# Eight gathers, then a look at the slab counter: GpSimd's rounds in layers two and three

## The chip, the cores and the metric

The kernel is one program on one core of a Trainium2 chip. Its time is the device time of one execution in microseconds (us), from the first to the last instruction. The kernel before takes 3301.0 us, the median of three runs (3299.79 to 3303.86).

## The reference

A graph of 6250 nodes (padded to 49 tiles of 128) and 200,000 edges with weights, features of 128. First a gated graph network of three layers, all in float32:

```python
for l in range(L):                      # L = 3
    m = x @ weight[l]
    msg = m[src] * edge_weight[:, None]
    agg = jax.ops.segment_sum(msg, dst, num_segments=N)
    x = _gru_cell(agg, x, w_ih, w_hh, b_ih, b_hh)
```

The result is added to the input and normalised over the features; then a second network of three layers, `relu((x + agg) @ W.T + b)` with an unweighted sum over the edges, is applied, added and normalised again.

## The kernel before

The sum over the edges is written as a product with a dense matrix. Layer one builds that matrix (weighted in `adj_w`, float32; counts in `adj_h`, float16) strip by strip, writes it to HBM and uses it at once. That takes the first 1090 us. The three count layers of the second network are the last 820 us. The change lies between them, in layers two and three.

The nodes are cut into 14 groups of 448 columns. In layers two and three the first 12 groups (`DENSE`) are dense: for each group TensorE multiplies the 49 tiles of node features `Y` with 49 pieces of the matrix, 128 x 448 float32, accumulating in one PSUM bank. A float32 product stands in the profile as two matmul records, so a group has 98 records of line 923 and the gates of a group 12 more (lines 933 to 936). The matrix of a group comes in four slabs (13, 12, 12 and 12 tiles, so 26, 24, 24 and 24 records). SyncE loads a slab into its buffer when the slab of the group before in that buffer has been used: the last matmul of each slab adds one to the semaphore `s_used` (line 925), and SyncE waits for it (line 511). `s_used` starts at 4. The order of TensorE is: the slabs of group g+1, then the gates of group g, then the slabs of group g+2. ScalarE copies the finished bank out (`evac`, line 1341, which also waits on `s_used`), computes sigmoids and tanh; VectorE does the rest of the cell (`mix` and `blend`, lines 1682 to 1696, "the cell update" below).

The sums of the last two groups are not made with the matrix. Their edges are handled in 350 rounds a layer (`ROUNDS`). In each round GpSimd gathers 128 rows of 512 bytes from `y_rows` in HBM with an indirect DMA into one of ten row buffers (`fetch_rows`, line 836, `ROW_BUFS` = 10), and VectorE adds the rows twice, with two weights, to the running sums (`add_rows`, lines 1738 and 1741). GpSimd may start round i when VectorE has finished round i - 10 (`s_acc`). VectorE's rounds are dealt over its cell updates by two constants, `SLOT_FIRST` = 30 and `SLOT_NEXT` = 33: 30 rounds at the start of the layer, and 33 after the cell update of each of the groups 0 to 8, 23 after that of group 9. "Slot s" below is the rounds 30 + 33 s to 62 + 33 s. VectorE runs slot s after the cell update of group s, which is while TensorE multiplies the slabs of group s + 2.

Nothing in the kernel before ties GpSimd's gathers to TensorE's progress except through VectorE. The order of the instructions on every engine is written out by hand.

Of the kernel before, what the change touches and what calls it, by code (L numbers as in the profile page):

```python
# [38 lines left out]
SLABS = len(SLAB_TILES)  # L39
# [13 lines left out]
DEALS = [(a // P, a % P, a, b - a) for a, b in zip(CUTS, CUTS[1:])]  # L53
DEALS += [(run, lane + REST, pair, n) for run, lane, pair, n in DEALS if run == RUNS - 1]
SLOT_FIRST, SLOT_NEXT = 30, 33
HALF_TILES = [(0, 25), (25, 49)]
HALVES = len(HALF_TILES)
HH = 25
# [40 lines left out]
def gnn_program(nc, x, src, dst, firsts, nodes, edges, edge_weight, gnn_w, w_ih, w_hh, b_ih, b_hh,  # L99
# [7 lines left out]
    with ctx:  # L107
# [3 lines left out]
        def sem(name):  # L111
            return ctx.enter_context(nc.semaphore(name))
# [128 lines left out]
        s_used = sem("s_used")  # L241
# [98 lines left out]
        s_mark_pool = sem("s_mark_pool")  # L340
# [30 lines left out]
        DENSE = GROUPS - 2  # L371
# [113 lines left out]
        def _(sp):  # L485
# [79 lines left out]
            with sp.If(fits):  # L565
# [16 lines left out]
                def stream_counts(l, i, r, s):  # L582
                    h0, h1 = HALF_TILES[s]
                    sp.wait_ge(s_used_h, HALVES * (GROUPS * l + 2 * i + r) + s + 1)
                    sp.dma_start(counts_slab(r, s)[:, :, 0:h1 - h0, :].rearrange("p u h c -> p u (h c)"),
                                 strips(adj_h)[:, bass.ds(2 * PARTS * i + PARTS * r, PARTS), h0 * SUB:h1 * SUB])\
                      .then_inc(s_slab_h[HALVES * r + s], 16)
# [66 lines left out]
        def _(pool):  # L654
# [170 lines left out]
            pool.wait_ge(s_steps, WIN * (GATHERS + 2))  # L825
            for buf in range(2):
                pool.wait_ge(s_near[buf], 16 * ((GATHERS + 4 - buf) // 2))
            def fetch_rows(layer):

                pool.wait_ge(s_rows, 2 * 16 * (layer + 1))  # L830
                for i in range(ROUNDS):
                    if i >= ROW_BUFS:
                        pool.wait_ge(s_acc, WIN * (ROUNDS * layer + i - ROW_BUFS + 1))
                    elif layer:
                        pool.wait_ge(s_acc, WIN * ROUNDS * layer)
                    pool.indirect_dma_start(out=run_rows[:, i % ROW_BUFS, :], out_offset=None, in_=y_rows,  # L836
                                            in_offset=bass.IndirectOffsetOnAxis(
                                                ap=run_edges[:, i, 0:1].bitcast(I32), axis=0))\
                        .then_inc(s_row[i % ROW_BUFS], 16)
# [3 lines left out]
            with pool.If(fits):  # L843
                for b in range(STRIPS_PER_GATHER):
                    pool.wait_ge(s_sh[b], 16 * (1 + GATHERS))
                for run in range(RUNS):
                    pool.indirect_dma_start(out=run_edges[:, run_cols(run), :].bitcast(I32).rearrange("p e k -> p (e k)"),
                                            out_offset=None, in_=edges,
                                            in_offset=bass.IndirectOffsetOnAxis(ap=run_take[:, run:run + 1], axis=0))\
                        .then_inc(s_list[run], 16)  # L850
                pool.wait_ge(s_mask, MASK_STEPS * RUNS)
                for layer in range(N_LAYERS - 1):
                    fetch_rows(layer)
# [16 lines left out]
        def _(pe):  # L870
# [243 lines left out]
            def halves_of_group(l, i, par, parts, fresh=False):  # L1114
                for s in parts:
                    h0, h1 = HALF_TILES[s]
                    pe.wait_ge(s_slab_h[HALVES * par + s], 16 * (PAIRS * l + i + 1))
# [1085 lines left out]
```

## Time and profile before

| | |
|---|---|
| median of three runs | 3301.0 us (3299.79 to 3303.86) |
| profiled execution, span | 3300.9 us |
| TensorE matmul busy | 2999.7 us, 91% |
| VectorE busy | 1519.5 us, 46% |
| GpSimd busy | 980.1 us, 30%, of it 673.5 us in the 700 gathers |
| mean granted TensorE clock | 0.941 of full speed |
| DMA | 796.32 MB, mean 241 GB/s |

The page gives no time for the profiled execution beside its span of 3300.9 us, which is the median of the runs to 0.1 us. "Busy" of TensorE counts matmuls whose ends are modelled. The granted clock has two levels here: 1.00 is 2.4 GHz, 0.50 is 1.2 GHz. A releaser named "issue" is time in which the engine waited for nothing that the profile can name.

### The profile page before, as it was taken

To read this page: it belongs to the slowest core of one execution; us is meant where nothing else is said; L and a number is where in the kernel's file an instruction comes from. 1 tells how busy PE (TensorE), PEld (TensorE's weight loads), DVE (VectorE), ACT (ScalarE), POOL (GpSimd) and SP (SyncE) were. 2 spreads that over 40 slices of the span, in tenths; PEclk is the share of its full clock that TensorE was granted. 3 is DMA by queue.
4 is the path that set the end of the run, shared out by engine and by line. 5 is a ranking of instruction groups with operands and counts; after the bars stand their busy time and mean duration, and the time that the engine had idled before them with its cause. 6 is when DMAs were issued, how large, how long until landed. Compare 5 with 4: busy or idle time off the path is not lost.

```text
span 3300.9 us, 75545 instructions
## 1 busy us (share of the span) xinstructions
PE 2999.7 (91%) x29405; PEld 1914.6 (58%) x29405; DVE 1519.5 (46%) x4507; ACT 904.4 (27%) x2115; POOL 980.1 (30%) x1214
## 2 busy tenths in 40 slices
PE   6999999999999987878789787878889999999998
PEld 5888888888888533434345333434345555555554
DVE  7888888888887233434342343434442001001111
ACT  5666666666665100000001001001022001001111
POOL 3222223222323344655551464554520000000000
PEclk8999999999999988878889888888889999999999
DMA  5655555555532866657577565746656876877885
GB/s 192 266 230 242 231 237 238 236 236 233 242 127 76 343 237 231 252 200 275 184 280 283 220 231 212 267 177 258 223 221 240 306 302 254 304 301 269 299 307 186
DMA packets 150125, 796.32 MB, mean 241 GB/s; under 512 B 19300, under 2 KB 29480, under 8 KB 136200
## 3 DMA queue, kind: packets, MB, share of 16 engines
q1 hardware_dynamic: 119960, 729.87, 56.3%
q0 software_dynamic: 27344, 54.53, 5.7%
q10 hardware_dynamic: 2720, 10.62, 0.8%
q8 instruction: 57, 0.93, 0.1%
q14 instruction: 44, 0.36, 0.0%
HBM read 567.97 MB, written 226.97 MB: 241 GB/s over the span
## 4 chain that ended last, share of the span: by engine, by line
PE 90%; issue 8%; DVE 1%; ACT 1%; DMA 0%; POOL 0%; another core or an unknown queue 0%; ACTq 0%; DVEq 0%; POOLq 0%
PE ps L923 28%; PE ps L1127 24%; PE ps L1206 18%; PE ps L1199 11%; PE ps L933 2%; PE ps L934 2%; PE ps L1219 1%; PE ps L935 1%; PE ps L936 1%; PE ps L1220 1%; PE ps L1106 1%; ACT ring L1602 0%; PE ps L1073 0%; PE ps L1221 0%; PE ps L1222 0%
## 5 line engine op out<-in xcount | busy, mean ns | idle before, releaser
L923 PE MATMUL ps<-ring,Y 128*128 128x448 f32 x2352 | 927.8, 550 | 145.6 <-issue 145.5
L836 POOL DMA_INDIRECT ring<-y_rows,ring x700 | 673.5, 962 | 683.4 <-DVE ring L1738 410.7
L923 PEld LDWEIGHTS ps<-ring,Y 128*128 128x128 f32 x2352 | 453.6, 193 | 594.8 <-issue 594.8
L1127 PE MATMUL ps<-ring,Y 128*128 128x448 f16 x4116 | 780.6, 352 | 0.0
L1602 ACT ACTIVATE ring<-ps 128x392 f16<-128x392 f32 (+1 forms) x1568 | 654.1, 504 | 303.6 <-PE ps L1199 297.1
L1127 PEld LDWEIGHTS ps<-ring,Y 128*128 128x128 f16 x4116 | 402.7, 98 | 373.8
L1206 PE MATMUL ps<-ring,Y 128*128 (+1 forms) x2744 | 613.9, 366 | 3.4 <-issue 2.9
L1738 DVE SCALAR_TENSOR_TENSOR ring<-ring 128x128 f32<-128x128 f32 x1384 | 402.1, 347 | 350.3 <-DMA ring<-y_rows,ring 223.8
L1206 PEld LDWEIGHTS ps<-ring,Y 128*128 128x128 f32 x2744 | 490.5, 189 | 19.3 <-issue 4.1
L1199 PEld LDWEIGHTS ps<-shared 64*128 64x128 bf16 x18816 | 341.3, 94 | 132.7 <-ACT ring L1602 87.0
L1199 PE MATMUL ps<-shared 64*128 64x49 bf16 (+1 forms) x18816 | 391.1, 191 | 22.4 <-issue 10.3
L2050 DVE TENSOR_TENSOR shared<-shared 128x400 bf16<-128x400 bf16 x1176 | 396.0, 391 | 0.0
L1341 ACT ACTIVATE shared<-ps 128x448 f32<-128x448 f32 x24 | 13.1, 544 | 1079.0 <-remote 847.8
L2046 DVE TENSOR_TENSOR shared<-iota_lo,shared 128x1024 bf16<-128x1024 bf16 x392 | 279.1, 712 | 0.0
L1914 DVE TENSOR_REDUCE x_tops<-xT x28 | 17.4, 620 | 482.3 <-ACT xT L1508 482.3
L1508 ACT ACTIVATE xT<-ps,bcur,unscale 128x448 f32 (+1 forms) x42 | 30.4, 725 | 682.1 <-PE ps L1127 682.1
L2044 DVE TENSOR_TENSOR shared<-iota_key,shared 128x400 bf16<-128x400 bf16 x392 | 148.1, 378 | 119.4 <-PE ps L1199 110.6
L1682 DVE SCALAR_TENSOR_TENSOR shared<-ps,bhh,shared 128x448 f32<-128x448 f32 x28 | 19.2, 684 | 329.0 <-ACT shared L1358 329.0
L731 POOL DMA_INDIRECT shared<-in_edges,take_now x60 | 61.8, 1029 | 360.0 <-PE ps L1199 357.3
L933 PE MATMUL ps<-shared,wT 128*128 128x448 f32 x112 | 78.5, 760 | 54.6 <-issue 53.8
L1880 DVE TENSOR_TENSOR shared<-shared,ps 128x384 f32 (+3 forms) x14 | 8.7, 622 | 228.5 <-PE ps L1142 228.1
L934 PE MATMUL ps<-xT,wT 128*128 128x448 f32 (+1 forms) x112 | 72.1, 720 | 27.6 <-issue 27.6
(188 smaller groups left out, 1309.6 us busy)
## 6 DMA issues: line engine op xcount, KB each, us to landing
ring<-adj_w SPq DMA_DIRECT2D x72, 2688.0 KB
adj_w<-ring SPq DMA_DIRECT2D x48, 2744.0 KB, 12.2
ring<-adj_h SPq DMA_DIRECT2D x42, 2800.0 KB, 9.4
ring<-adj_h SPq DMA_DIRECT2D x42, 2688.0 KB, 9.1
adj_h<-ring SPq DMA_DIRECT2D x56, 1372.0 KB, 5.0
ring<-adj_w SPq DMA_DIRECT2D x24, 2912.0 KB
ring<-y_rows,ring POOLq DMA_INDIRECT x700
y_rows<-Y ACTq DMA_DIRECT2D x2, 2560.0 KB, 10.9
```

The costliest lines, as they stand in the source:

```text
L836: pool.indirect_dma_start(out=run_rows[:, i % ROW_BUFS, :], out_offset=None, in_=y_rows, in_offset=bass.IndirectOffsetOnAxis(ap=run_edges[ ...
L923: mm = pe.matmul(ps[:, bank, 0:GW], Y[:, h, :], slab(s)[:, :, h - h0, :], start=(h == 0), stop=(last and h == TILES - 1))
L933: pe.matmul(ps[:, bank, 0:GW], wT[:, c, :], aggS[par], start=True, stop=False)
L934: pe.matmul(ps[:, bank, 0:GW], wT[:, 3 + c, :], xg, start=False, stop=True)
L1127: mm = pe.matmul(ps[:, par, 0:GW], part[:, h, :], counts_slab(par, s)[:, :, h - h0, :], start=(h == 0 and part is Y_high), stop=(h == TILE ...
L1199: mm = pe.matmul(sums, hot_lo[slots, buf, w, :], rhs, start=(part == 0), stop=(part == WPARTS - 1))
L1206: mm = pe.matmul(ps[:, AGG_BANK, 0:SPAN], Y[:, h, :], strip_w[:, bass.ds(slot, 1), :, h, :].rearrange("p o b c -> p (o b) c"), start=(h == ...
L1602: act.activation(strip[:, :, c0:c0 + UNIT * WIN].rearrange("p h (d j) -> p d h j", d=WIN), psum_unit(a)[:, :, kind, :, :].rearrange("p d j ...
L1738: add = dve.scalar_tensor_tensor(out=run_sums[:, run, d, :], in0=run_rows[:, buf, :], scalar=weight, in1=run_sums[:, run, d, :], op0=ALU.m ...
L2044: dve.tensor_tensor(in_pairs(hot[:, buf, :, 0, :]), every_window(iota_key, WIDE), values(par, 0, k, WIDE), ALU.is_equal).then_inc(s_hot, 1)
L2046: dve.tensor_tensor(in_pairs(hot_lo[:, buf, :, :]), every_window(iota_lo, P), values(par, 1, k, P), ALU.is_equal).then_inc(s_hot, 1)
L2050: dve.tensor_tensor(in_pairs(hot[:, buf, :, 1 + part, :]), in_pairs(hot[:, buf, :, 0, :]), values(par, 2 + part, k, WIDE), ALU.mult).then_ ...
```

## The change

Before the gather of the rounds 0, 8, 16, 24 and 32 of each slot, in both layers, GpSimd also waits on `s_used`. The threshold for round r of slot s is 4 (1 + 12 layer + s + 2) + r // 8 - 1 (`layer` is 0 for layer two and 1 for layer three). With the 4 at which the semaphore starts, that is 4 (s + 2) + r // 8 - 1 used slabs of this layer: for r = 0 the third slab of group s + 1, for r = 8 its fourth, for r = 16, 24 and 32 the first, second and third slab of group s + 2. The 30 rounds before slot 0 have no such wait. That makes 48 waits a layer, each followed by an increment of a semaphore that nobody waits for.

```diff
+ROUNDS_A_SLAB = 8
...
+            def slabs_before(layer, slot, r):
+                ahead = 2
+                return SLABS * (1 + DENSE * layer + slot + ahead) + r // ROUNDS_A_SLAB - 1
+
             def fetch_rows(layer):
 
                 pool.wait_ge(s_rows, 2 * 16 * (layer + 1))
...
                     elif layer:
                         pool.wait_ge(s_acc, WIN * ROUNDS * layer)
+                    slot, r = divmod(i - SLOT_FIRST, SLOT_NEXT)
+                    if slot >= 0 and r % ROUNDS_A_SLAB == 0:
+                        pool.wait_ge(s_used, slabs_before(layer, slot, r))
+                        pool.sem_inc(s_mark_pool, 1)
                     pool.indirect_dma_start(out=run_rows[:, i % ROW_BUFS, :], out_offset=None, in_=y_rows,
                                             in_offset=bass.IndirectOffsetOnAxis(
```

No instruction changes its place. On GpSimd's queue, from the gathers of the edge lists (`in_edges`) to the last round of layer three, the kernel before has these rows (`ring<-y_rows,ring` is one gather, with the semaphores for which it waits):

```order
L847 DMA ring<-in_edges,run_take 128x300 [waits s_sh1,s_sh0]
L847 DMA ring<-in_edges,run_take 128x300 x2
L847 DMA ring<-in_edges,run_take 128x150
L836 DMA ring<-y_rows,ring 128x128 [waits s_rows,s_mask]
L836 DMA ring<-y_rows,ring 128x128 x9
L836 DMA ring<-y_rows,ring 128x128 [waits s_acc] x340
L836 DMA ring<-y_rows,ring 128x128 [waits s_acc,s_rows]
L836 DMA ring<-y_rows,ring 128x128 [waits s_acc] x349
```

The changed kernel has, from the first gather of layer two to the first rounds of slot 1 (line 845 is the gather there):

```order
L845 DMA ring<-y_rows,ring 128x128 [waits s_rows,s_mask]
L845 DMA ring<-y_rows,ring 128x128 x9
L845 DMA ring<-y_rows,ring 128x128 [waits s_acc] x20
L845 DMA ring<-y_rows,ring 128x128 [waits s_acc,s_used]
L845 DMA ring<-y_rows,ring 128x128 [waits s_acc] x7
L845 DMA ring<-y_rows,ring 128x128 [waits s_acc,s_used]
L845 DMA ring<-y_rows,ring 128x128 [waits s_acc] x7
L845 DMA ring<-y_rows,ring 128x128 [waits s_acc,s_used]
L845 DMA ring<-y_rows,ring 128x128 [waits s_acc] x7
L845 DMA ring<-y_rows,ring 128x128 [waits s_acc,s_used]
L845 DMA ring<-y_rows,ring 128x128 [waits s_acc] x7
L845 DMA ring<-y_rows,ring 128x128 [waits s_acc,s_used] x2
```

The row of 340 gathers that waited for VectorE alone is now cut every eight gathers; the "x2" is round 32 of a slot and round 0 of the next, which wait for the same slab.

## Rows read from the trace of the kernel before

**Rows 1.** The page: chain that ended last, and the two costliest groups.
```profile
PE 90%; issue 8%; DVE 1%; ACT 1%; DMA 0%; POOL 0%; another core or an unknown queue 0%; ACTq 0%; DVEq 0%; POOLq 0%
...
L923 PE MATMUL ps<-ring,Y 128*128 128x448 f32 x2352 | 927.8, 550 | 145.6 <-issue 145.5
L836 POOL DMA_INDIRECT ring<-y_rows,ring x700 | 673.5, 962 | 683.4 <-DVE ring L1738 410.7
```
**Rows 2.** The chain in order of time, layers two and three: start, length, what.
```profile
1196.71 36.49 PE ps L923 x97
...
1254.06 35.84 PE ps L923 x95
1289.90 2.26 issue
1292.70 2.96 issue
...
1310.58 34.58 PE ps L923 x92
...
1713.10 27.81 PE ps L923 x74
...
1882.34 36.08 PE ps L923 x96
...
2411.57 27.81 PE ps L923 x74
```
**Rows 3.** Stretches: length, busy PE, PEld, DVE, ACT, POOL, clock, DMA share, GB/s.
```profile
1128.80:1144.10 15.30, 15.30 (x43) 7.68 (x42) 8.75 (x30) 0.54 (x1) 11.61 (x13) 1.00 0.82 312
1144.10:1173.40 29.30, 12.13 (x17) 4.31 (x16) 8.32 (x25) 0.00 (x0) 18.89 (x20) 0.59 0.18 45
1173.40:1196.70 23.30, 22.08 (x55) 10.90 (x54) 0.00 (x0) 0.54 (x1) 0.00 (x0) 0.93 0.98 393
...
1254.10:1310.60 56.50, 45.79 (x111) 21.81 (x110) 22.22 (x71) 2.28 (x4) 31.76 (x33) 0.88 0.62 230
...
1713.10:1754.40 41.30, 41.30 (x112) 20.86 (x112) 19.59 (x56) 3.47 (x6) 12.67 (x13) 1.00 0.99 402
```
**Rows 4.** SyncE's loads of slabs in time: start, length, count.
```profile
1264.11 0.38 SPq L512 DMA_DIRECT2D ring<-adj_w  x1
1273.02 0.37 SPq L512 DMA_DIRECT2D ring<-adj_w  x1
1306.36 0.99 SPq L512 DMA_DIRECT2D ring<-adj_w  x2
...
1173.48 2.61 SPq L512 DMA_DIRECT2D ring<-adj_w  x2
...
1741.07 0.37 SPq L512 DMA_DIRECT2D ring<-adj_w  x1
```
**Rows 5.** ScalarE in time, around the end of group 3.
```profile
1306.54 0.54 ACT L1341 ACTIVATE shared<-ps 128x448 f32<-128x448 f32 x1 [49.56 <-remote]
```
**Rows 6.** GpSimd's gathers in time; in brackets the idle time before.
```profile
1119.20 0.94 POOL L836 DMA_INDIRECT ring<-y_rows,ring  x1 [41.85 <-DMA y_rows<-Y]
...
1259.74 1.07 POOL L836 DMA_INDIRECT ring<-y_rows,ring  x1 [15.61 <-DVE ring L1738]
...
1285.25 1.01 POOL L836 DMA_INDIRECT ring<-y_rows,ring  x1 [0.30 <-DVE ring L1738]
1286.56 0.94 POOL L836 DMA_INDIRECT ring<-y_rows,ring  x1 [0.30 <-issue]
1287.81 0.95 POOL L836 DMA_INDIRECT ring<-y_rows,ring  x1 [0.30 <-issue]
...
1300.30 0.94 POOL L836 DMA_INDIRECT ring<-y_rows,ring  x1 [0.30 <-issue]
1316.49 1.09 POOL L836 DMA_INDIRECT ring<-y_rows,ring  x1 [15.24 <-DVE ring L1738]
```
**Rows 7.** VectorE in time, at the end of slot 1 and at its next cell update.
```profile
1291.56 0.35 DVE L1738 SCALAR_TENSOR_TENSOR ring<-ring 128x128 f32<-128x128 f32 x1 [1.12 <-issue]
1292.89 0.35 DVE L1738 SCALAR_TENSOR_TENSOR ring<-ring 128x128 f32<-128x128 f32 x1 [0.98 <-issue]
1311.46 0.68 DVE L1682 SCALAR_TENSOR_TENSOR shared<-ps,bhh,shared 128x448 f32<-128x448 f32 x1 [18.22 <-ACT shared L1358]
```

## The prediction, before the changed kernel was run

> **What bounds the kernel now.** I read the page's chain first: 90% of it is TensorE and 8% is "issue", time that no semaphore in the profile explains; the gathers (line 836) and the slab products (line 923) are the groups the change touches [rows 1]. Then the chain in order of time [rows 2]. In layers two and three it repeats once a group: some 95 matmul records of line 923 without a gap (35.84 us, 0.377 us each), and then a run of "issue" pieces of 2 to 3 us with one matmul between them, until the next group begins. The group that begins at 1254.06 is followed by the next at 1310.58. Over a layer that is a period of (1713.10 - 1196.71) / 9 = 57.38 us in layer two and (2411.57 - 1882.34) / 9 = 58.80 us in layer three. What it could be stands in the table by stretches [rows 3]: the last dense group, 1713.1 to 1754.4, does the same 112 records in 41.3 us at clock 1.00, and the DMA engines are then 0.99 busy. So each of 18 periods loses 16 to 17.5 us, and the first of each layer more: in 1144.1 to 1173.4 TensorE does 17 records in 29.3 us.
>
> What differs between the two kinds of group is GpSimd: 33 gathers in the one, 13 in the other [rows 3]. To see how that reaches TensorE, put SyncE's loads beside TensorE's slabs [rows 4]. The group that starts at 1254.06 ends its slabs after 26, 50, 74 and 98 records: about 1263.9, 1272.9 and 1282.0, the last in the stall. SyncE sends the loads that these free at 1264.11, 1273.02 and then both remaining ones at 1306.36. The third slab was done at 1282.0 and its count arrived 24.4 us later, together with the fourth. ScalarE, which waits on the same counter for the fourth, starts at 1306.54, after 49.56 us of idling [rows 5]. So TensorE's counts stop getting through between 1273 and 1282; from 1290 TensorE itself crawls, and VectorE starts one addition in 1.33 us (1291.56, 1292.89) where one takes 0.35 [rows 7]. GpSimd gathers from 1259.74 to 1300.30 without a break, then idles until 1316.49 [rows 6]; the count comes through 5.1 us after the last gather ended. From first gather to release is 46.6 us for 33 gathers, 1.41 us each, while GpSimd sends one in (1300.30 - 1259.74) / 32 = 1.27. At the layer's start it is 40 gathers from 1119.20 to the release at 1173.48: 1.36 each. In the last group, with 13 gathers, the third slab ends at 1713.10 + 27.81 = 1740.91 and its load goes out at 1741.07 [rows 2, 4]. My reading: a gather occupies something that all semaphore traffic needs for about 1.40 us; GpSimd feeds it faster than it clears, and after 14 to 22 us of unbroken gathering TensorE's counts are held until the backlog is gone.
>
> **What the change does, step by step.** It removes and moves nothing; it adds 96 waits on `s_used`, of which I price the wait instruction itself at nothing: GpSimd idles 15.6 us a group anyway [rows 6]. Behind a waiting gather stand only later gathers; VectorE's additions wait for those, behind them on VectorE the cell update of the next group, and for that TensorE's gates one group on.
>
> Where would the waits bite? By TensorE's own records hardly anywhere in mid-layer. Round 32 of slot 1 is the 23rd gather of its burst, sent at 1287.81 [rows 6]; the slab it would wait for was done at 1282.0, 5.8 us before. But the wait sees the count, and that arrived at 1306.3. So GpSimd stops after the gather of 1286.56, the 22nd. By 1.41 us a gather the backlog ends at 1259.74 + 31.0 = 1290.8, and the count comes through there, just when the stall would have begun (1289.90). The wait is on the very counter that is being starved, so it throttles the gathers when, and only when, they hold up TensorE.
>
> A group still needs 33 gathers. The nearest rows give these bounds for its period: not under 41.3 us, the free group; not over what it is now. If each gather holds the path for 1.41 us, 33 take 46.5 us, and TensorE's counts must pass between. GpSimd's own time for them is 33 x 1.27 = 41.9 us. I take 48.0 us: the 46.5 us and 1.5 us for what a shorter stall leaves, since the clock still falls to 0.50 when TensorE crawls (0.59 mean in the stall of 29.3 us) and comes back late [rows 3].
>
> - Layer two: 9 x (57.38 - 48.0) = 84 us.
> - Layer three: 9 x (58.80 - 48.0) = 97 us.
> - Start of each layer: round 30 now waits for seven used slabs. In the kernel before the burst ran to 40 gathers; now it is 30, whose backlog ends at 1119.20 + 30 x 1.40 = 1161 instead of 1173.4. 12 us in each layer, 24 us.
> - Rounds come later to VectorE. In a free group VectorE is busy 19.6 of 41.3 us, in the others 22.2 of 56.5 [rows 3], so it can take up rounds late by some us; after the last slot 23 rounds remain, 13 of them sent after VectorE begins, about as now. I put nothing for it; above, it costs when a slot's last rows come more than about 5 us after the group's last slab.
>
> Sum 84 + 97 + 24 = 205 us, from a profiled span of 3300.9, which is the median of the runs to 0.1: 3096 us. The loads of slabs are not the next bound: the free group moves its slabs at DMA share 0.99 in 41.3 us [rows 3], so at 48 us there is room, though not much.
>
> On the price of a count the trace and a rule part. The row: the third slab's count took 24.4 us from 1282.0 to SyncE, while the first two took 0.1 to 0.2 us [rows 4]. The Trainium skill, in "DMA: Bandwidth & Descriptors", section "Anatomy of one DMA — SWDGE (gpsimd) path", puts a semaphore update at about 100 ns, and "Advanced Engine Details and Errata", section "DMA Bandwidth Details", puts the overhead of an increment at about one cycle on trn2. By that rule the waits would be met long before they are reached and the kernel would stay near the first rival's time; by the rows above it gains 205 us. The first two slabs agree with the rule, the third does not.
>
> **The rivals.**
>
> *The waits do not bind in mid-layer.* The late counts might be an effect on SyncE and ScalarE alone, or GpSimd might see the counter where they do not. For: by TensorE's records the slab is done 5.8 us before round 32. Against: two other engines start within 0.2 us of each other at 1306.4 on this counter. Then only rounds 30 and 38 of each layer wait, and the time lies between no change and the 24 us of the starts: 3277 to 3301, say 3290.
>
> *There is no floor of 1.41 us a gather.* The backlog might come only from long unbroken bursts, and any pause clear it. For: 13 gathers in 16.3 us did no harm. Against: 33 gathers fit 46.6 us and 40 fit 54.3, near one rate. Then GpSimd's 41.9 us bound the period, and 18 periods give 9 x 15.5 + 9 x 16.9 = 292 us, with the starts 316: 2985.
>
> *The release is slow.* If the held counts need not the end of the backlog but the whole 5.1 us of quiet after a gather, and two waits a group pay it, the period is 41.9 + 10.2 = 52 to 54 us: 9 x 4.4 + 9 x 5.8 + 24 = 116 us at 53, 3185.
>
> *Slower: every wait pays.* GpSimd stops at four thresholds a group (32 and 0 share one). If each costs the 5.1 us from the last gather to the count, the period is 41.9 + 20.4 = 62.3 us, 4.9 and 3.5 us a period over now: 76 us more, less 24 at the starts: 3353. It decides from a pause of (57.4 - 41.9) / 4 = 3.9 us a wait. For: GpSimd has only 15.6 us of slack a group. Against: the first two thresholds of a fresh burst see counts that arrive in 0.2 us.
>
> **How the numbers follow.** The self-throttling case 0.61, predicted 3096, its own range 3060 (46 us a period) to 3150 (51 us). No floor 0.12. Slow release 0.11. Waits that don't bind 0.09, of which a third would still be over 0.2% faster. Slower 0.07. A difference of 0.2%, 6.6 us, is about what a measurement of this kernel can tell from none. Faster 0.61 + 0.12 + 0.11 + 0.03 = 0.87, the same 0.06, slower 0.07. The range that leaves out at most 2 in 10 goes from the no-floor case, 2990, to just above the slow release, 3215.
>
> **What the profile of the changed kernel would show.** The period of the line-923 stretches at 46 to 50 us in place of 57.4 and 58.8. GpSimd's idle time split over the group, with TensorE or `s_used` named as releaser of the gathers. No burst of gathers much over 25. SyncE's load for each third slab some 9 us after the slab, not 24. ScalarE's "remote" wait of line 1341 shrunk to match. "Issue" in the chain down from 8% to about 3%. The first stall of a layer ending near 1161 us. I am wrong if the period stays at 57 us with the waits met on arrival, or if VectorE's additions wait for rows for more than the present share and TensorE waits for the cell update.

## The result and the profile after

| | before | changed |
|---|---|---|
| median (range), four runs each | 3300.4 us (3296.7 to 3303.9) | 3136.4 us (3129.1 to 3152.8) |
| ratio, 95% interval | | 0.9512 (0.9483 to 0.9540) |
| profiled execution, span | 3300.9 us | 3132.8 us |
| mean granted clock | 0.941 | 0.971 |

The change makes the kernel 164 us faster by the medians, 168 by the spans. The prediction was 3096 us.

One thing must be known to read the numbers below: the chips on which the experiments ran are of two kinds. On two of them (numbers 3 and 13 below) the kernel before takes 3301 and 3321 us, as in the runs of the table, whose chip is not on record; on two others (6 and 10) the same kernel takes 2940 us. Each ratio is to the kernel before on the same chip.

The page of the changed kernel. After [rows 1] come the chain, the same two groups, and ScalarE's copy and VectorE's additions:

```profile
PE 93%; issue 4%; DVE 1%; ACT 1%; DMA 0%; POOL 0%; another core or an unknown queue 0%; ACTq 0%; DVEq 0%; POOLq 0%
...
L932 PE MATMUL ps<-ring,Y 128*128 128x448 f32 x2352 | 946.9, 560 | 103.0 <-issue 102.9
L845 POOL DMA_INDIRECT ring<-y_rows,ring x700 | 676.4, 966 | 516.0 <-issue 246.3
...
L1747 DVE SCALAR_TENSOR_TENSOR ring<-ring 128x128 f32<-128x128 f32 x1384 | 403.2, 347 | 402.4 <-DMA ring<-y_rows,ring 292.6
...
L1350 ACT ACTIVATE shared<-ps 128x448 f32<-128x448 f32 x24 | 13.1, 544 | 903.7 <-remote 515.7
```

Lines are nine higher than before (923 is now 932, 836 is 845). "Issue" fell from 8% to 4% of the chain. Of ScalarE's idle time before its copies 516 us end by "remote". The same two groups in the page of the kernel before:

```profile
L1738 DVE SCALAR_TENSOR_TENSOR ring<-ring 128x128 f32<-128x128 f32 x1384 | 402.1, 347 | 350.3 <-DMA ring<-y_rows,ring 223.8
...
L1341 ACT ACTIVATE shared<-ps 128x448 f32<-128x448 f32 x24 | 13.1, 544 | 1079.0 <-remote 847.8
```

So the additions now wait 69 us more for rows, and ScalarE 332 us less for a release that the profile calls "remote"; by [rows 4, 5] that is the counter `s_used`.

The chain of the changed kernel in order of time (start, length, what), to hold beside [rows 2]. First the start of layer two, then groups 2 and 3, then the last group of layer three:

```profile
1109.66 35.73 PE ps L932 x95
...
1160.26 20.11 PE ps L932 x47
...
1184.88 35.81 PE ps L932 x95
...
1227.35 23.30 PE ps L932 x62
...
1257.49 15.73 PE ps L932 x33
...
1277.73 36.83 PE ps L932 x98
...
2187.84 36.83 PE ps L932 x98
...
2229.18 2.63 PE ps L932 x7
2231.81 2.17 issue
2233.97 0.54 PE ps L932
2234.51 2.27 issue
...
2245.18 25.99 PE ps L932 x62
```

The first stall ends at 1160.26; the prediction said 1161. Groups of slabs start at 1184.9, 1227.4 and 1277.7: periods of 42.5 and 50.4 us. The last group, at 2229.18, stalls after seven records. In the kernel before the last group was free of stalls.

The stretches to hold beside [rows 3]: the period of 42.5, the one of 50.4, the last but one group of layer three, and the last. The columns are length, busy PE, PEld, DVE, ACT, POOL, clock, DMA share, GB/s.

```profile
1231.20:1273.70 42.50, 38.01 (x90) 18.21 (x89) 20.20 (x67) 0.36 (x1) 29.17 (x31) 0.88 0.79 296
1273.70:1324.10 50.40, 46.06 (x121) 22.89 (x120) 22.24 (x73) 1.92 (x4) 32.06 (x34) 0.98 0.75 280
2188.00:2229.30 41.30, 41.30 (x111) 20.90 (x110) 23.13 (x83) 5.88 (x12) 26.31 (x28) 1.00 0.89 337
2229.30:2281.30 52.00, 42.78 (x107) 20.70 (x106) 21.35 (x76) 4.05 (x7) 23.84 (x25) 0.87 0.67 249
```

28 gathers beside a group that does not stall at all, where before 33 cost 16 us: what matters is how they lie in time. Here is where GpSimd's gathers of the changed kernel begin after a pause, in answer to [rows 6] (in brackets the idle time; all others in this stretch stood 0.3 us behind the one before):

```profile
1222.46 0.95 POOL L845 DMA_INDIRECT ring<-y_rows,ring  x1 [3.85 <-remote]
1258.44 0.94 POOL L845 DMA_INDIRECT ring<-y_rows,ring  x1 [4.34 <-issue]
1290.65 1.10 POOL L845 DMA_INDIRECT ring<-y_rows,ring  x1 [8.59 <-DVE ring L1747]
1335.13 0.95 POOL L845 DMA_INDIRECT ring<-y_rows,ring  x1 [5.59 <-issue]
...
2202.26 1.07 POOL L845 DMA_INDIRECT ring<-y_rows,ring  x1 [6.96 <-DVE ring L1747]
```

The pauses cut the gathers into bursts of 25 (from 1222.46), 19 (from 1258.44) and 31 (from 1290.65); the burst before them is one of 22, from 1190.56. The burst of 31 from 2202.26 reaches over the start of the last group at 2229.18 and is what stalls it. SyncE's loads that the held counts of three bursts release:

```profile
1221.85 1.53 SPq L513 DMA_DIRECT2D ring<-adj_w  x2
...
1257.83 0.37 SPq L513 DMA_DIRECT2D ring<-adj_w  x1
...
1334.52 0.37 SPq L513 DMA_DIRECT2D ring<-adj_w  x1
```

From the first gather of the burst that is 31.3 us for 22, 35.4 for 25 and 43.9 for 31 gathers, 1.42, 1.41 and 1.42 us each. GpSimd starts again 0.6 us behind SyncE each time (1222.46, 1258.44 and 1335.13): it waits on the same held counter.

### The profile page after: what moved, and what is told of

Read it like the earlier page. It is cut to its first block, busy times and chain, and to the rows that moved or that the text cites. A ratio compares the mean times of both kernels' runs of the same rounds, so it can differ in the third digit from the quotient of the medians.

```text
span 3132.8 us, 75641 instructions
## 1 busy us (share of the span) xinstructions
PE 2965.1 (95%) x29405; PEld 1906.4 (61%) x29405; DVE 1519.6 (49%) x4507; ACT 903.4 (29%) x2115; POOL 983.2 (31%) x1214
## 3 DMA queue, kind: packets, MB, share of 16 engines
q1 hardware_dynamic: 119960, 729.87, 59.9%
## 4 chain that ended last, share of the span: by engine, by line
PE 93%; issue 4%; DVE 1%; ACT 1%; DMA 0%; POOL 0%; another core or an unknown queue 0%; ACTq 0%; DVEq 0%; POOLq 0%
PE ps L932 30%; PE ps L1136 25%; PE ps L1215 19%; PE ps L1208 11%; PE ps L942 1%; PE ps L943 1%; PE ps L1228 1%; PE ps L945 1%; PE ps L1229 1%; PE ps L944 1%; PE ps L1115 1%; PE ps L1231 0%; PE ps L1230 0%; PE ps L1104 0%; PE ps L1191 0%
## 5 line engine op out<-in xcount | busy, mean ns | idle before, releaser
L932 PE MATMUL ps<-ring,Y 128*128 128x448 f32 x2352 | 946.9, 560 | 103.0 <-issue 102.9
L1215 PEld LDWEIGHTS ps<-ring,Y 128*128 128x128 f32 x2744 | 490.4, 189 | 19.4 <-issue 4.1
L693 POOL COPY shared<-shared 112x128 f32<-112x128 f32 x28 | 13.6, 484 | 195.0 <-DVE shared L1982 195.0
L726 POOL TENSOR_SCALAR take_now<-steps_in,leap_start 112x2 int32<-112x2 f32 x30 | 30.1, 1004 | 114.1 <-DVE late L1958 113.4
```

The lines of the kernel that those rows point to most:

```text
L932: mm = pe.matmul(ps[:, bank, 0:GW], Y[:, h, :], slab(s)[:, :, h - h0, :], start=(h == 0), stop=(last and h == TILES - 1))
L1215: mm = pe.matmul(ps[:, AGG_BANK, 0:SPAN], Y[:, h, :], strip_w[:, bass.ds(slot, 1), :, h, :].rearrange("p o b c -> p (o b) c"), start=(h == ...
```

## What the experiments were to tell apart

The theory: a gather occupies what all semaphore traffic needs for about 1.40 us, GpSimd sends one in 1.25 to 1.27, and after some 20 unbroken gathers TensorE's counts are held until the backlog is gone. The rivals: it is the bytes or rows and not the gather; it is the burst and not the sum; it is the number of semaphore events of any kind; or the chip has nothing of the kind, and the cause of the stall lies elsewhere.

## First chip: no stall to explain

The first four ran on chip 6, where the kernel before takes 2940.4 us (25 runs).

**No gathers.** The gathers of rounds 10 and up are left out in both layers, and VectorE adds what stands in its buffers:

```diff
+                    if i >= ROW_BUFS:
+                        continue
...
-                    dve.wait_ge(s_row[buf], 16 * (len(range(buf, ROUNDS, ROW_BUFS)) * layer + i // ROW_BUFS + 1))
+                    if i < ROW_BUFS:
+                        dve.wait_ge(s_row[buf], 16 * (layer + 1))
```

> The kernel before, with the gathers of rounds 10 to 349 of both layers left out; VectorE still makes all its additions, on the rows of the first ten. Backlog theory: a burst of 10 gathers is harmless, so every dense group takes the free 41.3 us; the stretch from group 1 to the end of group 11 falls from 625.7 to about 454 us in layer two and from 634.2 to about 455 in layer three: 2950 us. Rival (the slow stretches come from VectorE's additions or from TensorE itself, such as a power limit after 35 us of float32 products): the periods stay at 57 to 59 us and the time at 3300.

Measured: 2933.3 us, ratio 0.9975 (0.9966 to 0.9985). All 680 missing gathers are worth 7 us here. The kernel before had no stall to lose.

**The first waits only.** Of the 96 waits, the two before rounds 30 and 38 of each layer stay:

```diff
+                    if slot == 0 and r <= 8 and r % ROUNDS_A_SLAB == 0:
```

> The changed kernel with only the waits of rounds 30 and 38 of each layer. Backlog theory: the first group of each layer ends its stall 11 us earlier as in the changed kernel, all later periods are those of before (57.4 and 58.8 us): 3300.4 - 22 = 3278 us. Rival (the gain comes from the later start of the slots' gathers, which then stays through the layer): near 3136 us.

Measured: 2940.2 us, ratio 1.0001 (0.9991 to 1.0010). Its trace is the clearest case against the theory as a general rule. Below are the stretch of a single burst, then SyncE's loads for the first, second and fourth slab of the group from 1150.19:

```profile
1155.90:1550.30 394.40, 394.40 (x1051) 199.32 (x1050) 209.26 (x674) 20.52 (x36) 300.13 (x310) 1.00 0.89 328
```
```profile
1160.24 0.38 SPq L513 DMA_DIRECT2D ring<-adj_w  x1
1169.15 0.37 SPq L513 DMA_DIRECT2D ring<-adj_w  x1
1187.19 0.37 SPq L513 DMA_DIRECT2D ring<-adj_w  x1
```

310 gathers without a break in 394.4 us, 1.27 each, and TensorE is busy in all of the 394.4 us. The fourth slab of that group ends at 1187.02 and the load goes out at 1187.19; no load in the whole burst goes out more than 0.3 us after its slab. By 1.40 us a gather a backlog of 40 us would have built up.

**Spaced gathers.** Each gather gets a memset of a small tile, with a semaphore of its own, ahead of it; one gather goes out each 1.33 us instead of each 1.25 (medians), less than the 1.45 to 1.5 that was aimed at:

```diff
+                    done = ROUNDS * layer + i
+                    if done:
+                        pool.wait_ge(s_pause, done)
+                    pool.memset(earlier[:, :], 0.0).then_inc(s_pause, 1)
```

> The kernel before, without any wait on used slabs; after every gather GpSimd sets a small unused tile to zero and waits for it, so that gathers leave it about every 1.45 to 1.5 us instead of 1.25. Backlog theory (a gather holds the path about 1.40 us): no backlog forms, TensorE's counts are never late, no stall, and the period is 33 gathers at this spacing, 48 to 49.5 us: 9 x 8.9 + 9 x 10.3 = 173 us less in the periods, plus up to 25 us at each layer's start: about 3100 us (3080 to 3140). Rival (what matters is that the waits listen to the starved counter, or that gathers keep out of certain slabs): spacing leaves the stalls, only slower gathers are added, 3300 us or more.

Measured: 2979.0 us, ratio 1.0132 (1.0115 to 1.0149). No stall was there to cure, but the price of slower gathers shows: the last group of layer two waits for its rows, and the layer's end takes 73.7 us instead of 54.8. The chain runs there over gathers and their landing, not over TensorE. What spacing does where there are stalls was not measured.

**Half the rows.** After the first ten of layer two a gather fetches 64 rows in place of 128:

```diff
-                    pool.indirect_dma_start(out=run_rows[:, i % ROW_BUFS, :], out_offset=None, in_=y_rows,
+                    pool.indirect_dma_start(out=run_rows[0:P // 2, i % ROW_BUFS, :], out_offset=None, in_=y_rows,
...
-                                                ap=run_edges[:, i, 0:1].bitcast(I32), axis=0))\
+                                                ap=run_edges[0:P // 2, i, 0:1].bitcast(I32), axis=0))\
```

> The kernel before, with each gather (but the first ten) fetching 64 rows instead of 128; the other half of the row buffer keeps old rows, so half of the sums is wrong; no wait is added. If the path is held per row (per descriptor), a gather holds it about 0.7 us, no backlog forms at any pace above that, and the periods are 41.3 us: near 2950 us, like the kernel without gathers. If it is held per gather (its 16 completions), nothing changes: 3300 us, or worse if the gathers leave GpSimd faster.

Measured: 2933.8 us, ratio 0.9977 (0.9967 to 0.9987). A gather goes out each 1.21 us instead of 1.25. Without a stall this tells nothing of its cause.

## Second chip: the change itself, and semaphore events

Chip 10; the kernel before takes 2940.7 us (27 runs).

**The changed kernel again**, unaltered.

> The changed kernel itself, once more. On the chip of the first four experiments the kernel before ran in 2940 us: there GpSimd gathers 310 rounds in one unbroken burst, every count arrives at once and every period is 41.3 us, so the stalls that the change shortened are not there. Theory now (the gain exists only where the counts are held up): here the waits are met 4 to 14 us before they are reached, so the ratio to the kernel before is 1.00 (0.998 to 1.003) if the chip is of the quick kind, and 0.95 if it is of the slow kind, where before takes 3300 us. Rival (the change itself costs or gains apart from the stalls): a ratio off 1.00 on a quick chip, for instance 1.01 because gathers, which need 41.25 of 41.3 us, are sent later.

Measured: 2940.8 us, ratio 1.0002 (0.9993 to 1.0011). The gain of 4.9% does not exist on this kind of chip. In its page TensorE's slab products have no idle time at all:

```profile
L932 PE MATMUL ps<-ring,Y 128*128 128x448 f32 x2352 | 888.4, 539 | 0.0
L845 POOL DMA_INDIRECT ring<-y_rows,ring x700 | 675.4, 965 | 350.3 <-issue 130.6
```

A gather takes 965 ns here and 966 in the page of the changed kernel above, so nothing in GpSimd's own work tells the two kinds apart.

**More events.** The kernel before, and after each load of a slab SyncE increments a semaphore that nobody waits for 60 times:

```diff
+                for _ in range(60):
+                    sp.sem_inc(s_mark_sp, 1)
```

> The kernel before; SyncE additionally increments an unused semaphore 60 times after each of the 96 slab loads of layers two and three, some 3 us of every 9. Theory that the hold-up is a saturated path for semaphore events (and their records): with this added traffic the counts come late and the slow stretches return also on a quick chip, over 3000 us. Rival (the hold-up belongs to the gathers and something of the other machine): 2940 us on a quick chip.

Measured: 2942.9 us, ratio 1.0008 (0.9998 to 1.0018). The increments of SyncE in a stretch of layer two in which 193 gathers go out (count, then the duration of one in ns: least, median, most):

```profile
L517 SPq EVENT_SEMAPHORE  x1440: 17/17/17, 1160.2 to 1397.4; - x180
```

1440 increments, not one slower than 17 ns, in the midst of gathers.

**One slab later.** The changed kernel with each threshold raised by one:

```diff
-                return SLABS * (1 + DENSE * layer + slot + ahead) + r // ROUNDS_A_SLAB - 1
+                return SLABS * (1 + DENSE * layer + slot + ahead) + r // ROUNDS_A_SLAB
```

> The changed kernel with every threshold one slab later (the even pace itself). Where counts are prompt, a slot's gathers of rounds 16, 24 and 32 now wait 2 to 5 us once, then stay in step; the rows come up to 5 us later and the end of the layers has that room: 2940 to 2950 us. Where counts are held up (before 3300 us): GpSimd stops sooner after TensorE, the bursts of 31 gathers disappear, periods of 46 to 47 us, 3100 us against 3136.

Measured: 2947.4 us, ratio 1.0023 (1.0014 to 1.0033): 6.6 us slower, since rows come later to the last cell updates of a layer (the end of layer two takes 55.7 instead of 54.8 us, the last group of layer three 40.5 instead of 37.8) and nothing is gained.

## Third chip: the same increments where the stalls are

Chip 13; the kernel before takes 3320.7 us. Two kernels with more events: SyncE adds 120 increments after each load of a slab, and ScalarE 250 after each `update`.

```diff
+                for _ in range(120):
+                    sp.sem_inc(s_mark_sp, 1)
...
+                for _ in range(250):
+                    act.sem_inc(s_mark_act, 1)
```

**Many events on the kernel before.**

> The kernel before with far more semaphore events in layers two and three: SyncE 120 increments of an unused semaphore after each slab load, ScalarE 250 after the tanh of each group in its loops, 0.058 us each as measured in the kernel with 60. Together with the gathers' 16 completions each this is up to 50 events a microsecond, against 16 in the kernel before. Theory (the slow kind of machine has a path for semaphore events or their records with too little capacity; the quick kind has more, but a limit too): counts come late and periods grow well over 41.3 us, the more so where both engines increment. Rival (it is not the number of events): 2940 us, or up to 20 us more where ScalarE's increments delay its own copies.

Measured: 3714.8 us (two runs), ratio 1.1194 (1.1153 to 1.1236); periods of 78.5 us in layer two. The same view of SyncE's increments, first for 29 us in which no gather runs, then for 36.8 us inside a burst, and the two stretches (columns as above):

```profile
L518 SPq EVENT_SEMAPHORE  x383: 17/17/17, 1262.0 to 1291.0; - x192
```
```profile
L518 SPq EVENT_SEMAPHORE  x32: 6/700/727, 1300.1 to 1336.8; - x32
```
```profile
1262.00:1291.00 29.00, 21.15 (x51) 10.71 (x52) 3.61 (x7) 2.28 (x4) 0.00 (x0) 0.79 0.83 318
1300.00:1336.80 36.80, 13.88 (x37) 6.51 (x35) 11.67 (x36) 0.00 (x0) 24.85 (x27) 0.75 0.18 47
```

This shows the hold-up on an engine that has nothing to do with the gathers: an increment that takes 17 ns while GpSimd is idle takes 700 ns while it gathers. The first slow one starts at 1292.75, 1.3 us after the first gather of the burst (1291.43), the last at 1336.79, and from 1338.2 on they are quick again. That is 46.8 us after the first gather, for 33 gathers: 1.42 each, the rate of the backlog once more. Between these times SyncE starts one increment each 1.4 us for the most part. It is not the price of a gather by itself, since this kernel adds increments of two engines to the gathers; in the kernel before the first two counts of a burst still take 0.1 to 0.3 us.

In a stall TensorE goes forward in the same unit: 0.54 and 2.27 us in the rows from 2233.97 above are 2.81, four times 0.70. In layers two and three of the kernel before 137 of the 152 steps of more than 1 us from one matmul record to the next lie within 0.025 us of 1.40, 2.10, 2.80 or 3.50, two to five times 0.70.

The Trainium skill, "DMA: Bandwidth & Descriptors", section "Anatomy of one DMA — SWDGE (gpsimd) path", gives about 100 ns for the semaphore update with which a DMA ends. No run here times that update by itself. SyncE's own increments take 17 ns beside no gathers and throughout on chip 10, and seven times the page's figure inside a burst on chip 13.

**Many events on the changed kernel.** The same increments added to it.

> The changed kernel with the same added events. If the added events hold up the counts, the waits of GpSimd thin its gathers and the changed kernel is faster than the one before with the same events, by at least 1%; if not, both are equal within 0.2%.

Measured: 3610.9 us (two runs), ratio 1.0881 (1.0847 to 1.0916) to the kernel before, so 0.972 of the kernel with many events and without the change. Periods of 71.3 and 74.9 us (means over nine). The change still helps with the path that full, by less.

## Fourth chip: the gathers where the stalls are

Chip 3; the kernel before takes 3301.0 us (8 runs). Three of the kernels above were run again here.

**Half the rows.**

> The kernel before with 64 rows in place of 128 in each gather after the first ten of a layer: half the rows and bytes, the same number of gathers. On a chip where the kernel before takes 3300 us or more (the kind on which both records of the comparison were made): if the price is paid per gather (completions), 3290 to 3310 with periods of 57 us, ratio 0.99 to 1.00; if it is paid per row or per byte, the 1.40 us a gather become about 0.70, the backlog never forms, periods of 41.3 us, about 2950, ratio 0.89 to 0.92. On a chip where the kernel before takes 2940: 2934 as before, which tells neither apart.

Measured: 3323.8 us, ratio 1.0062 (1.0042 to 1.0082). It is the gather and not the row: half the rows and half the bytes save nothing. The burst that begins at 1256.91, its last gather, and SyncE's next two loads, of which the first was held:

```profile
1256.91 1.04 POOL L842 DMA_INDIRECT ring<-y_rows,ring  x1 [16.43 <-DVE ring L1744]
...
1297.20 0.91 POOL L842 DMA_INDIRECT ring<-y_rows,ring  x1 [0.94 <-remote]
```
```profile
1303.52 1.41 SPq L512 DMA_DIRECT2D ring<-adj_w  x2
```

From first gather to release: 46.61 us for 33 gathers, 1.41 each. In [rows 6, 4] it is 1306.36 - 1259.74 = 46.62. It is 0.6% slower than before, above the 3290 to 3310 us expected; the periods are 58.6 and 59.2 us against 57.4 and 58.8. Why they are longer I did not find out.

**No gathers.**

> The gathers of the rounds from 10 on are left out in both layers, and VectorE adds what stands in its buffers. On a chip of the 3300 kind: if the gathers alone make its stalls, all periods are 41.3 us and the time is 2933 to 2960, ratio 0.89 to 0.90, which is the most that any order of the gathers could give; if the slow kind has another cause besides, it stays above 3000. On a chip of the 2940 kind: 2933, ratio 0.9975.

Measured: 2952.1 us, ratio 0.8943 (0.8923 to 0.8963). All periods are 41.3 to 42.1 us, and TensorE's line is that of the other kind of chip:

```profile
L925 PE MATMUL ps<-ring,Y 128*128 128x448 f32 x2352 | 888.4, 539 | 0.0
```

So the gathers alone make the whole difference in these layers: 3300.9 - 2948.8 = 352 us by the spans, of which the change brings back 168. Layer one, which this edit leaves alone, takes as long as before to 2 us. What still lies between this time and the 2933.3 us of the same kernel on chip 6 arises there: the first slab product of layer two starts at 1087.9 us here and at 1071.2 on chip 6. Its cause was not looked for.

**One slab later.**

> The changed kernel with each threshold one slab later. On a chip of the 3300 kind: if the leftover loss of the changed kernel is bursts let through because GpSimd lags its thresholds by 12 to 22 us, the later thresholds break them up: no burst over 20, periods of 43 to 46 us where the changed kernel has 48.6 and 49.2, and 3060 to 3110, ratio 0.925 to 0.94; if the price is 1.40 us a gather wherever it stands, periods stay at 48 to 50 us and the ends of the layers are dearer by some us: 3135 to 3160, ratio 0.95 to 0.957. On a chip of the 2940 kind: 2947, ratio 1.002.

Measured: 3112.9 us (3111.9 to 3115.8), ratio 0.9427 (0.9406 to 0.9448). It beats the changed kernel, whose interval to the same 3300 us begins at 0.9483; no run of that one on this chip is on record. On chip 10 it was the slower by 0.2%. By the starts of its groups the periods are 46.3 us in layer two and 48.6 in layer three, against 48.6 and 49.2. The gain is smaller than expected (3060 to 3110 us), since bursts of 22 to 25 remain and, in layer three, two of 31. GpSimd's first gathers after a pause, and SyncE's loads at the same places:

```profile
1196.30 0.94 POOL L845 DMA_INDIRECT ring<-y_rows,ring  x1 [4.26 <-issue]
1219.61 0.94 POOL L845 DMA_INDIRECT ring<-y_rows,ring  x1 [3.64 <-issue]
1244.36 0.94 POOL L845 DMA_INDIRECT ring<-y_rows,ring  x1 [3.61 <-issue]
1278.92 0.94 POOL L845 DMA_INDIRECT ring<-y_rows,ring  x1 [4.47 <-DVE ring L1747]
```
```profile
1219.01 0.37 SPq L513 DMA_DIRECT2D ring<-adj_w  x1
...
1243.87 2.55 SPq L513 DMA_DIRECT2D ring<-adj_w  x2
...
1278.32 0.37 SPq L513 DMA_DIRECT2D ring<-adj_w  x1
```

These rows give the size of the backlog for short bursts. 16 gathers from 1196.30 are released at 1219.01, 17 from 1219.61 at 1243.87, 24 from 1244.36 at 1278.32: 22.7, 24.3 and 34.0 us, 1.42, 1.43 and 1.41 us each. With 33 it is 1.41, of either size. GpSimd again starts 0.5 to 0.6 us after SyncE. And the bursts of 16 and 17 stall nothing, as the chain of this kernel shows (two groups at full speed, the third stalled by the burst of 24):

```profile
1185.75 36.83 PE ps L932 x98
...
1227.09 36.83 PE ps L932 x98
...
1268.43 2.63 PE ps L932 x7
1271.06 2.06 issue
```

In most of the longer bursts of both kernels TensorE's matmuls first fall behind 24 to 31 us after the first gather, some 20 to 24 gathers in. Bursts of 16 to 19 with a pause behind them that lasts until the release delay no matmul.

## Why the prediction was right, and where it was off

- **The wait bites, and on the starved counter.** Right. By the end of its matmuls the slab was done before the gather was reached at 94 of the 96 waits, at 92 of them 3.6 to 17 us before; yet GpSimd idles 3.4 to 5.6 us at 19 of them, until the held count arrives. So the rival in which the waits do not bind is refuted. So is the slower one, in which all four of a period pay 5.1 us: there are 19 such pauses in the two layers, about one a period, and they are as long as the backlog is (24 gathers sent in 30.1 us and released after 34.0: 3.9; for 16 gathers it is 3.0, for 33 it was 5.1). That fits no fixed price of a release either, the third rival. The kernel before already spoke against it: at the start of layer two the last of the forty gathers ends at 1173.33, and the count comes at 1173.48 [rows 4]. That burst, too, is less plain than I read it: its last seven gathers came in pieces, as VectorE freed buffers, so its 1.36 us each is no rate of a full burst.
- **1.40 us a gather.** Right on this kind of chip, now for bursts of 16 to 33, with pauses between them; so there is a floor, against the second rival. As I wrote it, as what a gather does, it is wrong: on chips 6 and 10 a gather does nothing of the kind.
- **Period 48.0 us.** The nine periods run from 1184.7 to 1622.4 in layer two, 48.63 each, and from 1786.2 to 2229.0 in layer three, 49.2 each: gains of 78.7 and 86.4 us where 84 and 97 were forecast. But it is no even 48: layer three settles into pairs of 60.8 and 41.3 us. A burst of 31 goes out with thresholds already met, since GpSimd is up to 17 us behind them, and stalls a group; the next is free.
- **Starts of the layers.** 11.1 and 10.6 us gained, 12 each forecast. The stall ended 0.7 us from where 1.40 x 30 puts it.
- **No burst much over 25.** Wrong: 31, in the pairs above, and 30 at the start. With bursts of 22 and 25 one count a group is 9 to 13 us late, near the 9 forecast, though with 25 it is mostly the second slab's and not the third's; with 31 it is the fourth slab's, 20 to 21 us late.
- **The end of a layer, which I priced at nothing.** This is the term that was mis-sized. From the start of the last dense group of layer two to the next layer is 59.9 us, 54.8 before; the last group of layer three takes 52.0 us, 37.8 before. In the kernel before, the last groups had 13 gathers beside them; now bursts of 25 and 31, pushed later by the waits, reach into them. That costs 5.1 + 14.3 = 19.4 us. I had looked at the 23 rounds after the last slot and not at what the waits push there.

The sum: 78.7 + 86.4 + 21.7 - 19.4 = 167.4 us, against 168.1 by the spans. Of the 38 us between the 205 forecast and this sum 19 are the layers' ends, 16 the periods and 2 the starts. So the mechanism was right, and two terms of the sum were too favourable.

What stays open is what the two kinds of chip differ in. Each chip was used in one session, so it is not shown either that a chip stays in its kind. One trace of the changed kernel holds 26,958 semaphore updates (chip 10), the other 16,222. Of the 10,736 missing ones 8831 belong to the ten semaphores that the gathers of layers two and three increment: 1109 to 1118 records each on chip 10, of 1120 that there must be, against 176 to 284. But counters of other engines have gaps too: VectorE's `s_acc` has 807 records against 1401, and the four semaphores of SyncE's slab loads 67 to 182 against 377 to 385. The increments themselves did arrive, or VectorE and TensorE would have stood still; their records are missing. Every run here, the timed ones too, has a span and a clock read from such records. So it may be the recording of a gather's sixteen increments that is too slow on these chips and holds up the others behind it, and not the increments themselves. A run without any recording would tell; it wasn't tried. Nor was a fixed spacing of the gathers, or the change with its first waits only, measured on a chip with stalls. So it is shown that shorter bursts stall less, and that the waits on `s_used` make them shorter; whether waits on that counter do it better than any even spacing is not.

## What to carry to other kernels

When TensorE stalls for nothing that the profile names, put the time at which each count was made beside the time at which its waiters start: if several engines start together, long after, the path is late and not the work. Then ask how long the bursts of small indirect DMAs are, not how many there are: up to some 20 in a row delayed no matmul here, and a wait on the progress of the engine to be protected, chosen so that no burst grows beyond that even when GpSimd lags, was worth more than halving the bytes. Measure it on more than one chip: here the same change was worth 4.9% on one kind and nothing on the other.

## What the runs showed of the hardware

- Four chips, two speeds: the unaltered kernel takes 2940.4 and 2940.7 us on two, 3301.0 and 3320.7 on two others, 12 to 13% more, with a mean granted clock of 0.99 in the one case and 0.94 in the other. The gathers of two layers make all but 19 us of the difference: without them the kernel takes 2952.1 us on chip 3 and 2933.3 on chip 6.
- On the slower kind an increment of a semaphore by SyncE takes 17 ns beside no gathers and 700 ns inside a burst of them; 64 or 128 rows in a gather make no difference to the backlog, 1.41 us a gather.
- On the faster kind 310 gathers in a row, one each 1.27 us, delay no count by more than 0.3 us.
